# A router that chooses on the logits and counts with TensorE, feed-forward scales with a second tensor operand, and start-up constants spread over five steps

## The reference, cut to what matters

```
scale = max(max(|xb|) / 6, 1e-12);  q = GRID[searchsorted(MID, |xb / scale|)] * sign(xb) * scale
y = (silu(q(x) @ q(Wg).T) * (q(x) @ q(Wu).T)) quantised again, @ q(Wd).T
```

## Time and profile before

| what | us |
|---|---|
| three timed runs: median (lowest to highest) | 1427.94 (1427.52 to 1429.84) |
| the profiled execution: its own time | 1431.45 |
| the profiled execution: its span, first to last instruction | 1429.7 |
| TensorE busy | 1108.4 (78%) |
| VectorE busy | 930.1 (65%) |
| ScalarE busy | 823.5 (58%) |
| GpSimd busy | 640.4 (45%) |

### The profile page before, as it was taken

One profiled execution on the slowest core, in us unless ns is written; L12 is line 12 of the kernel. 1 busy time (PEld: TensorE's weight loads), 2 busy tenths in 40 slices (PEclk: granted clock), 3 DMA queues, 4 the chain that ended last, 5 costly groups with the idle time before them and its releaser, 6 DMA issues.

```text
span 1429.7 us, 33712 instructions
## 1 busy us (share of the span) xinstructions
PE 1108.4 (78%) x11264; PEld 857.8 (60%) x11265; DVE 930.1 (65%) x1715; ACT 823.5 (58%) x1442; POOL 640.4 (45%) x922
## 2 busy tenths in 40 slices
PE   0577659999986776489999915899998737999991
PEld 0355536666653555279999903455555416999991
DVE  5799748888947998833333356889998384333333
ACT  0455326777764553366666562677767625666665
POOL 3322254444401222047766604666776403777660
PEclk9999959999997999679999956999999956999995
DMA  8100023222210000111111132442233010111115
GB/s 251 42 1 0 1 48 66 53 63 65 52 22 1 1 0 1 59 32 49 48 46 47 44 119 60 73 78 62 60 73 77 3 59 21 50 47 47 47 47 184
DMA packets 160689, 74.96 MB, mean 52 GB/s; under 512 B 125451, under 2 KB 152852, under 8 KB 160596
## 3 DMA queue, kind: packets, MB, share of 16 engines
q1 hardware_dynamic: 151508, 55.06, 16.0%
q0 software_dynamic: 9088, 18.63, 4.4%
HBM read 28.03 MB, written 15.73 MB: 31 GB/s over the span
## 4 chain that ended last, share of the span: by engine, by line
PE 51%; DVE 26%; issue 8%; ACT 5%; DMA 4%; POOL 2%; SPq 2%; DVEq 1%; POOLq 0%; ACTq 0%
PE PS L1011 18%; PE PS L1039 9%; PE PS L668 4%; DVE m L794 4%; PE PS L634 3%; PE PS L596 3%; PE PS L650 2%; DVE q_amax L273 2%; SPq L896 2%; DVE fscale L288 2%; PE PS L622 2%; DMA qT<-qs 2%; DVE sg L794 2%; PE PS L676 2%; DVE bn L188 1%
## 5 line engine op out<-in xcount | busy, mean ns | idle before, releaser
L1011 PE MATMUL PS<-xTs,pt 128*128 128x128 f32 x2272 | 280.9, 278 | 0.0
L1011 PEld LDWEIGHTS PS<-xTs,pt 128*128 128x128 f32 x2272 | 269.5, 195 | 0.0
L742 ACT ACTIVATE pt<-PS 128x768 f32<-128x768 f32 (+1 forms) x256 | 225.8, 915 | 49.6 <-PE PS L596 23.7
L1156 DVE TENSOR_TENSOR pt<-pt,PS 128x512 f32<-128x512 f32 x142 | 97.6, 688 | 233.8 <-PE PS L1011 183.8
L1284 POOL DMA_INDIRECT xs<-rows,src x142 | 138.1, 972 | 152.3 <-DVE src L1150 109.6
L1073 ACT ACTIVATE pt<-wgu 128x1024 f32 x142 | 150.0, 1058 | 87.8 <-issue 80.8
L1294 POOL DMA_INDIRECT outs<-ys,dst x142 | 140.3, 988 | 93.7 <-DVE ys L1171 86.6
L794 DVE TENSOR_REDUCE m<-PS 128x4 f32<-128x1024 f32 x128 | 153.4, 1221 | 27.7 <-PE PS L596 25.1
L1039 PE MATMUL PS<-wdn,pt 128*128 x1136 | 150.3, 275 | 1.2 <-DVE ys L1171 1.2
L794 DVE TENSOR_REDUCE sg<-PS 128x6 f32<-128x768 f32 x128 | 118.1, 954 | 32.5 <-PE PS L596 30.8
L1039 PEld LDWEIGHTS PS<-wdn,pt 128*128 128x128 f32 x1136 | 138.0, 192 | 1.7 <-issue 1.7
(11 more groups left out here) (241 smaller groups left out, 2188.5 us busy)
## 6 DMA issues: line engine op xcount, KB each, us to landing
pt<-outs SPq DMA_DIRECT2D x16, 512.0 KB, 4.9
rows<-qT SPq DMA_DIRECT2D x12, 256.0 KB, 2.2
xs<-rows,src POOLq DMA_INDIRECT x142, 2.5
outs<-ys,dst POOLq DMA_INDIRECT x142, 2.3
wgu<-in_L_ffn_w_gate SPq DMA_DIRECT2D x1, 2048.0 KB
wgu<-in_L_ffn_w_up SPq DMA_DIRECT2D x1, 2048.0 KB
wdn<-in_L_ffn_w_down SPq DMA_DIRECT2D x8, 256.0 KB
out<-X SPq DMA_DIRECT2D x8, 256.0 KB, 4.6
```

Source lines behind the costliest of these rows:

```text
L742: s.activation(k.pt[:, a % 4, :, 0:w], k.PS[:, self.bank:self.bank + 2, 0:w], ACT.Exp, scale=self.scale).then_inc(self.s_p, 1)
L1011: last = t.matmul(k.PS[:, 1 + 2 * p + w, c * P:(c + 1) * P], k.wst[:, 1 - p, w, c * P:(c + 1) * P], k.xTs[:, p, :], start=True, stop=True)
L1156: v.tensor_tensor(k.hs[:, p, :], k.sgs[:, p, :], k.PS[:, 2 + 2 * p, :], ALU.mult).then_inc(self.s_h, 1)
```

## The change

**Routing.** The choice is made on the logits after the subtraction (the largest is 0) and no longer on their exponents; the exponent is taken of the second largest alone. The first choice is found with a reversed index table (`riota`), made at the start of the routine together with a table of which expert lies below which (`less`). TensorE multiplies `chosen` by a single column of ones, which puts each (tile, expert) count on a partition; VectorE copies the counts out, spread over 128 columns, in bfloat16 (exact, they are at most 128); four more matmuls with a constant 0/1 table (`earlier`) give the experts' totals (bank 4) and add the counts of earlier tiles to the ranks in bank 5. The sum over the experts is a product with `less` and one reduction.

**Feed-forward scales.** L288 becomes a `scalar_tensor_tensor` whose second tensor, `least`, is filled with -1e-12 at the start.

**Constants.** What GpSimd made in one piece after step 1 is spread over steps 1 to 5, each after that step's own L324, with one more cast (`earlier`, 528 columns) and one more load in SyncE's row of later weights. The low-rank products move from the end of the first feed-forward stage to its step 1, in bank 7, on TensorE after L376 and on ScalarE after the silu; TensorE's first use of bank 7 for results, in step 3, waits for them.

```diff
+def constants(g, ch, k, z):
+    if z == 1:   # iota2, tileb, memset of bias, and
+        ch.run(g.tensor_copy(k.earlier[:, :, :].rearrange("p h c -> p (h c)"), k.eload))
+    elif z == 2: # bpart <- bload; bias row 0
+    elif z == 3: # bload -= bpart; bpart <- bload
+    elif z == 4: # bias row 32; bload -= bpart
+    elif z == 5: # bias row 64
...
-            ch.run(v.tensor_scalar(scale, amax, -1.0 / 6.0, -1e-12, ALU.mult, ALU.min))
+            ch.run(v.scalar_tensor_tensor(scale, amax, -1.0 / 6.0, k.least[:, b], ALU.mult, ALU.min))
...
-            if self.constants and isinstance(z, int) and z == 1:
-                self.constants()
+            if self.constants and isinstance(z, int) and 1 <= z <= 5:
+                eng.wait_ge(self.s_xq, z + 1)
+                if h:
+                    eng.wait_ge(self.s_hq, z - 2)
+                self.constants(z)
...
         eng.wait_ge(self.s_mask, 1)
-        t.matmul(k.PS[:, 5, 0:NT * NE], k.before[:, :], k.chosen[:, :], start=True, stop=True)
-        t.matmul(k.PS[:, 6, 0:NT * NE], k.onesb[:, :], k.chosen[:, :], start=True, stop=True).then_inc(self.s_rank_ps, 1)
+        for h in range(2):
+            last = t.matmul(k.PS[:, 6, h:h + 1], k.chosen[:, h * P:(h + 1) * P], k.onesb[:, 0:1], start=True, stop=True,
+                            skip_group_check=True)
+        last.then_inc(self.s_cnt_ps, 1)
+        t.matmul(k.PS[:, 5, 0:NT * NE], k.before[:, :], k.chosen[:, :], start=True, stop=False, skip_group_check=True)
+        eng.wait_ge(self.s_cnt, 1)
+        for h in range(2):
+            t.matmul(k.PS[:, 4, 0:NE], k.cnt[:, h, :], k.earlier[:, h, NT * NE:], start=h == 0, stop=h == 1)
+        for h in range(2):
+            last = t.matmul(k.PS[:, 5, 0:NT * NE], k.cnt[:, h, :], k.earlier[:, h, 0:NT * NE], start=False, stop=h == 1,
+                            skip_group_check=True)
+        last.then_inc(self.s_rank_ps, 1)
...
-        s.activation(k.ex[:, :, :], k.lg[:, :, :], ACT.Exp).then_inc(self.s_e, 1)
+        s.activation(k.ratio[:, :], k.top[:, 1, :], ACT.Exp).then_inc(self.s_e, 1)
...
+        ch.run(last)
+        ch.run(v.scalar_tensor_tensor(kk, lg, 0.0, riota, ALU.is_ge, ALU.mult))
+        ch.run(v.tensor_reduce(k.mx[:, :], kk, AX.X, ALU.max))
+        ch.run(v.tensor_tensor(oh[:, 0, :, :], riota, bc(k.mx[:, :]), ALU.is_equal))
+        ch.run(v.scalar_tensor_tensor(rest, oh[:, 0, :, :], -1e30, lg, ALU.mult, ALU.add))
+        v.tensor_reduce(k.top[:, 1, :], rest, AX.X, ALU.max).then_inc(self.s_lg, 1)
+        eng.wait_ge(self.s_lg, 1)
+        ch.run(v.tensor_tensor(kk, rest, bc(k.top[:, 1, :]), ALU.is_ge))
+        ch.run(v.tensor_tensor(kk, kk, riota, ALU.mult))
+        ch.run(v.tensor_reduce(k.mx[:, :], kk, AX.X, ALU.max))
+        ch.run(v.tensor_tensor(oh[:, 1, :, :], riota, bc(k.mx[:, :]), ALU.is_equal))
...
+        eng.wait_ge(self.s_cnt_ps, 1)
+        v.tensor_copy(k.cnt[:, :, :], k.PS[:, 6, 0:2].unsqueeze(2).broadcast_to([P, 2, P])).then_inc(self.s_cnt, 1)
+        eng.wait_ge(self.s_e, 1)
+        # 1 + ratio, its reciprocal, times 0.5, times ratio: four instructions on 32 columns
         eng.wait_ge(self.s_rank_ps, 1)
...
+        # nt: three instructions on 8 columns, the first from bank 4
+        ch.run(v.tensor_tensor(k.below[:, :, :], k.less[:, :, :], nt.unsqueeze(1).broadcast_to(square), ALU.mult))
+        ch.run(v.tensor_reduce(starts, k.below[:, :, :], AX.X, ALU.add))
+        ch.did(v.tensor_tensor(ends, starts, nt, ALU.add))
+        ch.run(v.tensor_scalar(starts, starts, float(P), None, ALU.mult))
+        ch.run(v.tensor_tensor(rest, k.PS[:, 5, 0:NT * NE].rearrange("p (t e) -> p t e", e=NE),
+                               starts.unsqueeze(1).broadcast_to([P, NT, NE]), ALU.add))
+        for r in range(2):
+            ch.did(v.tensor_tensor(oh[:, r, :, :], oh[:, r, :, :], rest, ALU.mult))
+        ch.settle()
+        ch.run(v.tensor_reduce(k.top[:, :, :], oh[:, :, :, :], AX.X, ALU.add))
```

More of the change, by code:

```diff
@@ L212, in __init__ @@
         self.q0 = run * (self.N + 3)
-        self.constants = None
+        self.constants = self.copies = self.products = None
         self.s_xn = k.sem("ffn_xn")
@@ L377, in fn @@
                 last.then_inc(self.s_up_ps, 1)
+            if self.products and isinstance(z, int) and z == 1:
+                self.products()
             if h:
+                if self.products and isinstance(z, int) and z == 3:
+                    eng.wait_ge(self.k.sem("low_rank_product_copied"), 1)
                 eng.wait_ge(self.s_hqT, x0 + z - 2)
@@ L440, in fn @@
                 s.activation(k.sg[:, :, :], k.PS[:, 0:2, 0:I0], ACT.Silu).then_inc(self.s_silu, 1)
+            if self.copies and isinstance(z, int) and z == 1:
+                self.copies()
         self.walk(eng, fn)
@@ L1225, in route @@
+        ch.did(v.tensor_tensor(k.wt[:, 1, :], k.ratio[:, :], k.wt[:, 0, :], ALU.mult))
         eng.wait_ge(self.s_rank_ps, 1)
[L1227 to L1235, removed]
@@ L1237, in route @@
-        nt, e0, e1 = k.small[:, 0, :], k.small[:, 1, :], k.small[:, 2, :]
-        ch.run(v.tensor_scalar(nt, a[:, NT - 1, :], P - 1.0, 1.0 / P, ALU.add, ALU.mult))
+        nt, ends, starts = k.small[:, 0, :], k.small[:, 1, :], k.small[:, 2, :]
+        ch.run(v.tensor_scalar(nt, k.PS[:, 4, 0:NE], P - 1.0, 1.0 / P, ALU.add, ALU.mult))
         ch.run(v.tensor_scalar(nt, nt, -(0.5 - 1.0 / 256), ROUND, ALU.add, ALU.add))
         ch.run(v.tensor_scalar(nt, nt, ROUND, None, ALU.subtract))
-        ch.run(v.tensor_copy(e0, nt))
@@ L1242, in route @@
[L1242 to L1251, removed]
@@ L1261, in route @@
                                       ALU.mult, ALU.add))
-        return e0
+        return ends
     def experts(self, eng, ch, e0):
@@ L1339, in __init__ @@
             sb(n, [P, NT]) for n in ("veps", "mean", "std", "rstd", "nt", "nmr"))
-        self.gone, self.one = sb("gone", [P, 1]), sb("one", [P, 1])
+        self.gone, self.one, self.least = sb("gone", [P, 1]), sb("one", [P, 1]), sb("least", [P, (2 * D + 2 * I0) // BLK])
         self.ident, self.identb = sb("ident", [P, P]), sb("identb", [P, P], BF16)
@@ L1499, in _ @@
             load(k.lists[:, :], a["lists"])
+            load(k.eload, a["earlier"])
             load(k.wgu[:, 0], a["L1_ffn_w_gate"].rearrange("e d f -> d e f"))
@@ L1533, in _, with constant @@
             dequantise(nc, k.wq, k.qt, (0, k.NW), (s_wm, 1), s_wq)
[L1535 to L1541, removed]
+            def constant(z):
+                if z == 1:
+                    pool.wait_ge(s_w2, 16 * NW_LOADS)
+                constants(nc.gpsimd, ch, k, z)
+                if z == 5:
+                    pool.sem_inc(s_bias, 1)
+            kinds[0].constants = constant
             for i, ph in enumerate(kinds):
@@ L1594, in _, with low_rank @@
             pe.wait_ge(s_wT, 1)
+            def low_rank():
+                pe.wait_ge(s_w2, 16 * NW_LOADS)
+                nc.tensor.transpose(k.PS[0:QL + KVL, 7, 0:P], k.wa[:, :], k.ident[:, :]).then_inc(s_waT_ps, 1)
+                pe.wait_ge(s_waT, 1)
+                nc.tensor.matmul(k.PS[:, 7, P:P + D], k.waT[0:QL, :], k.wb[0:QL, 0:D], start=True, stop=True)
+                nc.tensor.matmul(k.PS[:, 7, P + D:P + D + 96], k.waT[QL:QL + KVL, :], k.wb[QL:QL + KVL, D:D + 96],
+                                 start=True, stop=True).then_inc(s_wab_ps, 1)
+            kinds[0].products = low_rank
             for i, ph in enumerate(kinds):
```

80 lines of the change are left out of this document (36 added, 44 removed).

## The result

The changed kernel takes 1416.01 us (median of four runs, 1414.93 to 1417.09) against 1428.83 for the kernel before on the same chip (also four runs). By the medians that is 12.8 us less; the ratio of the runs, 0.9903 with a 95% interval of 0.9875 to 0.9931, gives 13.9 less (9.9 to 17.9). The forecast was 1414.1, range 1408 to 1420. The profiled execution took 1415.85, span 1414.1.

The account below looks back on a forecast made before the run. The chain of waits was half TensorE, a quarter VectorE, so edits were judged by stage: routing 11.4, constants 2.2, stage end 1.0, minus scales 0.8, is 13.8 us; from 1427.94 that gives 1414.1, range 1408 to 1420.

Parts of the forecast that it names:

- Routing: VectorE's uncovered chain from the second subtraction to the list: 11.02 instead of 16.76 us a layer, 11.4 less for both.
- The round trip: Routing, after `chosen`: VectorE waits for TensorE's two matmuls with one moving column, 0.40 us, bounds 0.25 and 0.9.
- the four small ones: Routing, behind the copy: four small VectorE instructions instead of five, about 0.9 us, covering TensorE's four matmuls.
- the tail: Routing, VectorE's remaining instructions after the four small ones, through the unchanged last five: together 4.46 us.
- one element a step: Routing: the reduction of 512 columns costs the 256-column one plus 0.27, so 0.72 us.
- Scales: Feed-forward loop: the new scale form is held beside GpSimd like the old, costing 0.8 us more, bounds -0.3 and +1.5.
- Rival 1: Feed-forward loop: the new scale form is not held, the 17.5 us comes whole, 1395.8 us; chance 0.04.
- Constants: Start of first feed-forward stage: GpSimd's constants cost 3.9 us; spread, with 0.7, 0.7 and 0.3 given back, 2.2 less.
- 0.7 is left after the slack of ScalarE: First feed-forward stage: low-rank products in step 1 delay TensorE about 1.5 us, of which 0.7 remains, bounds 0 and 1.5.
- Step 4: First feed-forward stage: the constants' long GpSimd subtraction starts right behind L324 and holds VectorE's L290, costing 0.7 us.
- step 5: First feed-forward stage: the constants' other subtraction on GpSimd runs late and meets L312, costing 0.3 us.
- 11 to 12 us: Sign named for the start: L312 of step 3 comes some 11 to 12 us behind L324 of step 1.

Follow-up runs that it names:

- the routing alone: Only the new routing, with old scales, constants in one piece and low-rank products at the stage's end: 1416.42 us against 1427.58 for the kernel before, ratio 0.9927.
- the scale-only kernel: The kernel before with only the new form of the scale: 1428.97 us against 1427.58, ratio 1.0014.
- the two PSUM kernels: Changed kernel from step 2 with the scale's second operand in PSUM, 1396.94 us; or old scale, largest magnitudes and reciprocals in PSUM, 1399.52 us.
- the start-only kernel: The kernel before with only the constants spread over steps 1 to 5 and low-rank products in step 1: 1426.13 us against 1427.58, ratio 0.9984.
- the changed kernel's second execution: The changed kernel run again with no further edit: 1415.81 us against 1427.58 for the kernel before, ratio 0.9921.
- the counter-test: The changed kernel with low-rank products back at the first feed-forward stage's end, constants still spread: 1416.90 us against 1429.49 for the kernel before, ratio 0.9903.

## Why the prediction was right

- **Routing, forecast 11.02 a layer, measured 10.86.** `chosen` ends 4.87 after the subtraction (forecast 4.86). The round trip is 0.30 (0.40), the copy 0.34 (0.40), the four small ones 0.92 (0.90), the tail 4.43 (4.46). Counting starts of instructions of known width on one engine was good to 0.2 in 11, and the routing alone gives the change's time within what these runs resolve. Its "one element a step" stands for what two rows show, 0.42 us for 256 columns (L1210) and 1.16 for 960 (L313), which is 1.05 ns a column; the reduction of 512 columns was worth 0.72 from start to start (0.72), and the new scale form took 0.22 (0.22) for 60 columns in the one step in which GpSimd was idle, step 3 of the second feed-forward stage. The ends of its range were added up a little wrong (round trips 0.5 and 0.7 worse are 1.2 and not 1.1 in a layer; 0.15 better makes 5.9 and not 6.1); nothing hangs on that.
- **Scales, forecast 0.8 more.** Right: held, and 0.02 to 0.03 a step; the two stages of the scale-only kernel are 1.0 longer. (The working's 38 times 0.03 is 1.1; its 0.8 is 26 times 0.03.) Rival 1 (free, 1395.8) was turned down for the right reason, L805's 0.61 beside GpSimd against 0.19 at its shortest; that the hold is one of SBUF operands is now shown by the two PSUM kernels: beside GpSimd's product the new form took 0.22 with one of its two operands in PSUM and 0.93 with both in SBUF. Two SBUF tensors are not the whole condition, though: the old form has one and is held (0.89), the reciprocal has one too and is not (0.53 beside GpSimd's product and 0.53 behind it). The runs show that a PSUM input frees the old form as well (0.22), not what sets it apart from the reciprocal.
- **Constants, forecast 2.2 less; the rows give 3.4** (3.0 from step 0 to step 18, and 0.4 of scales on top), in the start-only kernel 2.7, where TensorE's slower products of step 1 cost the half us. The mechanism held, but the terms were off. What the constants had cost was put too low: with the products at the end the stretch from step 1 to step 3 is 9.09, less than the 9.64 of the second stage that the forecast took for it, so 4.5 and not 3.9. The low-rank products cost 0.1 (0.7): the step that failed is "0.7 is left after the slack of ScalarE", for the slack took all but 0.1 of the 1.5. Step 4 was right, 0.73 (0.7). In step 5 the rounding loses 0.05 (0.3); by their lengths steps 5 and 6 lose 0.13 and 0.08 (7.60 and 7.40 in the first stage of the changed kernel's second execution, 7.47 and 7.32 in its second stage). So 4.5 - 0.1 - 0.7 - 0.2 is about the 3.4 of the rows. Of the marks that I named for it, "11 to 12 us" from step 1 to step 3 was wrong too, and did not fit the forecast of 3.9 less with 0.7 back (10.4); it is 9.19.
- **End of the stage, forecast 0.9 to 1.0 less.** 0.9 from the last statistics to the next mean, with the products back as the counter-test.
- **The sum, forecast 13.8.** The rows add up to 11.8 + 3.4 + 0.9 - 0.8 = 15.3. The times say 12.8 by the medians and 13.9 by the ratio, and 11.8 and 11.3 for the changed kernel again; the three parts alone come to 10.4 + 2.3 - 2.0 = 10.7 by the ratio. That the forecast came so near is in part luck: the start gives 1.2 more than it had and the routing 0.4 more, and the late half clock of TensorE was in none of its terms. In the profile of the changed kernel that clock costs 3.4 (from the scale of step 18 to the next mean 14.62, against 11.22 in the second execution). That it accounts for the gap between rows and times is not shown: the two profiled executions differ by 15.6 in spite of it, and the first attention, which no edit touches, is 2.2 shorter in that of the changed kernel (254.15 against 256.37). From 160 to 174 the granted clock was 0.52 in three of the five profiles with spread constants and the scales held, 0.87 and 0.88 in the other two, and 0.88 in the three with the constants in one piece and the scales held. Whether the earlier start makes the low clock likelier there stays open: three of five against none of three is too little to tell.

## What to carry to other kernels

A row that is several times longer in a loop than alone (here 0.89 against 0.19), and that ends just behind another engine's instruction (0.05 to 0.08), is probably held and not at work: try where its operands lie before you try its form. Here the form cost 1 to 2 us, and the place of 60 numbers was worth 17 on the kernel before and 20 to 22 on the changed one. On a chain that nothing covers, add up starts by operand width and cut instructions; a round trip to an idle TensorE cost 0.30 of waiting, and counting through it saved 4.43 us in each layer.

## What the runs showed that I had not expected

- I had priced a free scale at 17.5 by the scale rows alone, though the scaled values behind it have two SBUF tensors and could have been held in its place. In the loop they are not: scale and reciprocal (0.22 + 0.53 and gaps) fill the time until GpSimd ends to within 0.13, and the scaled values take 1.16 as they do alone. That this is the reason is argued from the rows, not tested.
- The hold works both ways: GpSimd's subtraction takes 2.20 instead of 1.40 when VectorE's scaled values came first, and 1.41 when these read one of their two tensors from PSUM.
- One program's executions lie 10 us apart (1408.91 to 1418.99), and stages that no edit touched differ too: the second attention took between 292.9 and 297.0 over the twelve profiles. TensorE's granted clock was 0.93 in the shortest and 0.91 in the longest, but 0.93 also in the 296.6 of the changed kernel's profile, so that the clock is the reason is not shown. An edit worth 2 us has to be read from its own rows.
